# Four fused transformer layers on one core: a 64-column recurrence, first loads split over two queues, new order tables

## What is computed

```
x = L0(x, ctx)    # self-attention (16 heads of 64, causal) + cross-attention + FFN, three layer norms
x = L1(x, ctx)    # attention with 16 heads of 8, masked rows
x = L2(x, ctx)    # linear attention: one encoder layer on ctx, one decoder layer (8 heads of 16), FFNs
x = L3(x, ctx, base)   # attention with 8 heads of 16, then a recurrence over the 128 tokens
# the recurrence inside L3
U = (layernorm(x) @ W_in.T + b_in) @ Bmat
def step(s, u_t):                      # s is [32, 64]
    s = silu(s @ A.T) + u_t
    return s, s
_, states = scan(step, zeros, U)       # 128 steps, each needs the one before
out = x + einsum('tbs,sh->bth', states, Cmat) + mod
```

## Time and profile before

| | us |
|---|---|
| median of three runs | 2123.61 |
| profiled execution | 2124.64 |
| its span | 2122.9 |
| PE busy | 1872.6 (88%), 13625 matmuls |
| PE weight loads busy | 1198.0 (56%) |
| DVE busy | 1339.7 (63%) |
| ACT busy | 1109.4 (52%) |
| POOL busy | 239.0 (11%) |

### The profile page before, as it was taken

One profiled execution on the slowest core, in us unless ns is written; L12 is line 12 of the kernel. 1 busy time (PEld: TensorE's weight loads), 2 busy tenths in 40 slices (PEclk: granted clock), 3 DMA queues, 4 the chain that ended last, 5 costly groups with the idle time before them and its releaser, 6 DMA issues.

```text
span 2122.9 us, 36204 instructions
## 1 busy us (share of the span) xinstructions
PE 1872.6 (88%) x13625; PEld 1198.0 (56%) x13625; DVE 1339.7 (63%) x3612; ACT 1109.4 (52%) x3858; POOL 239.0 (11%) x263
## 2 busy tenths in 40 slices
PE   5887998899988998899988998899988998877699
PEld 2555565646655565546655565556655566544345
DVE  3554768577775768577775768577775768554410
ACT  3452845557363845557363845567473836433222
POOL 0001011010212011010212011010202011010000
PEclk9999999999999999999999999999999999988999
DMA  6000000000000000000000000000000000000001
GB/s 196 1 1 6 12 1 1 1 17 2 1 1 6 12 2 1 1 17 1 1 1 6 13 1 1 1 17 2 1 2 6 1 1 1 1 1 1 1 16 25
DMA packets 25138, 20.14 MB, mean 9 GB/s; under 512 B 2243, under 2 KB 22790, under 8 KB 24966
## 3 DMA queue, kind: packets, MB, share of 16 engines
q1 hardware_dynamic: 24966, 17.83, 2.9%
HBM read 15.73 MB, written 2.10 MB: 8 GB/s over the span
## 4 chain that ended last, share of the span: by engine, by line
PE 54%; DVE 23%; ACT 17%; issue 4%; POOL 2%; SPq 1%; DMA 0%; POOLq 0%; DVEq 0%; ACTq 0%
PE ps L825 12%; PE ps L833 11%; ACT probs L1474 7%; PE ps L873 5%; ACT s_probs L1474 4%; PE ps L974 3%; PE ps L897 3%; DVE neg_max L1735 3%; DVE tok L1755 3%; DVE stats L1742 3%; PE ps L883 2%; PE ps L998 2%; PE ps L1422 2%; PE ps L869 2%; PE ps L821 2%
## 5 line engine op out<-in xcount | busy, mean ns | idle before, releaser
L1474 ACT ACTIVATE probs<-ps,neg_max 128x128 f32<-128x128 f32 x1024 | 362.2, 395 | 147.7 <-DVE neg_max L1735 146.5
L1474 ACT ACTIVATION_READ_ACCUMULATOR probs<-ps,neg_max 128x1 f32 x1024 | 238.8, 234 | 0.0
L1474 ACT ACTIVATE s_probs<-ps,s_max 128x128 f32<-128x128 f32 x672 | 183.7, 396 | 95.6 <-DVE s_max L1735 95.6
L1735 DVE TENSOR_REDUCE neg_max<-ps 128x4 f32<-128x512 f32 x256 | 164.5, 684 | 89.8 <-PE ps L873 89.8
L647 POOL TENSOR_TENSOR rstd<-var_eps,minus_half 128x4 f32<-128x4 f32 x88 | 94.4, 1072 | 1068.0 <-DVE var_eps L1748 1067.2
L1742 DVE BATCH_NORM_STATS2 stats<-ps 128x6 f32<-128x128 f32 x352 | 78.2, 284 | 181.4 <-PE ps L833 179.6
L1777 DVE TENSOR_TENSOR probs<-probs,inv 128x512 f32<-128x512 f32 x256 | 177.1, 692 | 8.8
L1468 ACT ACTIVATE probsT<-ps 128x512 f32<-128x512 f32 (+1 forms) x270 | 164.2, 629 | 27.3 <-PE ps L883 13.6
L883 PE MATMUL ps<-ident,probs 128*128 128x128 f32 x1024 | 156.5, 281 | 8.6 <-ACT queries L1468 4.6
L873 PEld LDWEIGHTS ps<-keys,queries 64*128 64x128 f32 x2048 | 125.7, 189 | 54.7 <-issue 54.7
L873 PE MATMUL ps<-keys,queries 64*128 64x128 f32 x2048 | 150.5, 287 | 0.0
(11 more groups left out here) (296 smaller groups left out, 3421.8 us busy)
## 6 DMA issues: line engine op xcount, KB each, us to landing
x_in<-in_x SPq DMA_DIRECT2D x8, 256.0 KB, 3.0
c_in<-in_ctx SPq DMA_DIRECT2D x8, 256.0 KB, 3.2
skip_in<-in_mask_BxS_ik SPq DMA_DIRECT2D x8, 256.0 KB, 3.1
out<-headsT SPq DMA_DIRECT2D x28, 64.0 KB, 1.8
valid_in<-in_mask_BxS_bf SPq DMA_DIRECT2D x8, 64.0 KB, 3.7
w_qkv_sa<-in_L_xattn_sa_wq SPq DMA_DIRECT2D x1, 512.0 KB
w_qkv_sa<-in_L_xattn_sa_wk SPq DMA_DIRECT2D x1, 512.0 KB
w_qkv_sa<-in_L_xattn_sa_wv SPq DMA_DIRECT2D x1, 512.0 KB
```

The lines of the kernel that those rows point to most:

```text
L1474: last = A(dst[:, u % dst.shape[1], h * 128:h * 128 + 128], bank(st, (tag, "s", u))[:, h * 128:h * 128 + 128], ACT.Exp, bias=src_max[:, u ...
L1735: V.tensor_reduce(dst[:, u % 2, :], bank(st, (tag, "s", u)).rearrange("p (h k) -> p h k", h=4), AX.X, ALU.max, negate=True).then_inc(max_r ...
```

## The change

Three parts.

- **Recurrence.** All matmuls of it get weights of 64 columns: `scan_step` (only the 64 columns of `aT` that matter), the filler (`keep_half`), the states and the residual. The last two now take two time steps each in place of four and write 64 partitions of the bank, alternating between the lower and the upper half, so there are 64 of each in place of 32. The residual is no longer a transposition but an ordinary matmul with the identity. Even steps carry the states, odd steps the residual and a filler of 512 columns; the 768-column filler is gone but for the first step.
- **First loads.** The self-attention weights are loaded in halves (k, q and v of the first heads ahead of ctx, the rest behind), each with its own semaphore. The 8 vectors that are needed first, and the mask, are issued on ACT's queue; the other 26 stay on SP behind the self-attention weights. `col_rows` is transposed in two parts, the first before main step 1, the second before step 12. x, ctx and the mask have a semaphore each. ACT waits for the set-up steps only before its first projection, not before its first copy.
- **Order tables.** `MAIN_ORDER` and `SIDE_AT` are replaced. They hold the same items and the same 87 steps. They serve all eight passes.

```diff
-MAIN_ORDER = ("i0 av00 aq0 mk ak0 aq1 as0 ak1 av10 aq2 av01 as1 av11 av02 ax0 ak2 i1 ax1 aq3 ax2 at0 at1 as2 "
-              "av03 ak3 av12 ak4 ax3 at2 aq4 ax4 ao0 ax5 at3 as3 av13 ao1 ax6 at4 at5 ax7 aq5 at6 as4 ak5 aq6 "
-              "ao2 ak6 ax8 ax9 at7 as5 ao3 at8 ax10 at9 ax11 as6 ak7 ax12 aq7 at10 ao4 ax13 at11 as7 cv00 cv01 "
-              "ax14 ao5 at12 ax15 at13 cv02 at14 ao6 at15 ao7 y1 ck0 ck1 r1 n1 cv10 cv11 cq0 cv12 cs0 cv03 cx0 "
-              "cv13 cq1 cx1 cq2 ck2 cs1 ct0 cx2 ct1 cx3 cs2 cq3 ck3 co0 cq4 ct2 ct3 cx4 cx5 ck4 cs3 ck5 ct4 co1 "
-              "ct5 cx6 cx7 cs4 cq5 ck6 cx8 co2 cx9 ct6 cq6 ct7 ct8 cs5 cq7 co3 ct9 cx10 cs6 ck7 cx11 cx12 ct10 "
-              "co4 cx13 ct11 cs7 co5 cx14 cx15 ct12 ct13 ct14 co6 ct15 co7 y2 r2 n2 f0 f1 f2 f3 y3 r3 n3").split()
+MAIN_ORDER = ("i0 ak0 mk aq0 as0 av00 ak1 i1 ax0 av10 aq1 ax1 at0 as1 av01 av02 at1 ax2 ak2 aq2 av03 at2 as2 "
+              "ax3 ak3 ak4 ao0 aq3 ax4 av11 aq4 ax5 at3 as3 ao1 av12 av13 at4 at5 ax6 as4 ak5 ax7 ak6 at6 ao2 "
+              "aq5 at7 ax8 as5 ax9 ax10 aq6 ao3 at8 at9 at10 as6 ak7 ax11 aq7 cv00 ao4 at11 ax12 as7 cv01 ax13 "
+              "ao5 ax14 at12 at13 ax15 ck0 ao6 at14 at15 ao7 cv02 y1 cv10 ck1 r1 cv11 n1 cv12 cq0 cs0 cv03 cx0 "
+              "cq1 ck2 cx1 cv13 cs1 ck3 cx2 cq2 cq3 ct0 cx3 ct1 ct2 cs2 co0 ck4 cq4 cx4 ct3 cs3 co1 cq5 cx5 ck5 "
+              "ct4 cx6 ct5 cx7 cs4 ct6 cq6 co2 cx8 ct7 ct8 ck6 cs5 cx9 co3 ck7 cx10 ct9 cs6 cx11 co4 cq7 cx12 "
+              "ct10 ct11 cx13 cs7 co5 ct12 cx14 ct13 ct14 cx15 co6 ct15 co7 y2 r2 n2 f0 f1 f2 f3 y3 r3 n3").split()
...
-SIDE_AT = (0, 3, 4, 5, 8, 8, 10, 10, 12, 15, 16, 19, 21, 24, 26, 29, 33, 40, 42, 48, 49, 53, 56, 59, 62, 65,
...
+SIDE_AT = (3, 3, 4, 6, 6, 10, 14, 17, 18, 20, 20, 24, 27, 28, 30, 33, 39, 43, 48, 49, 53, 55, 55, 59, 62, 63,
...
+            load_x(0)
+            for c in "kqv":
+                load_sa(c, 0)
+            load_context(0)
+            for c in "kqv":
+                load_sa(c, 1)
+            for c in [*COLUMN_WIDTH][len(COLUMNS):]:
+                sp.dma_start(column_rows(c), column_source(c)).then_inc(loaded_vectors, 16)
...
-            pe.wait_ge(consts_ready, n_const[0])
-            pe.wait_ge(loaded_first, n_first[0])
-            nc.tensor.transpose(ps[:, 5, 0:NCOLS], col_rows[:, :], ident[0:NCOLS, 0:NCOLS]).then_inc(setup_filled, 1)
+            pe.wait_ge(consts_ready, IDENT_STEPS)
+
+            def turn_columns():
+
+                pe.wait_ge(consts_ready, n_const[0])
+                pe.wait_ge(loaded_columns, 16 * len(COLUMNS))
+                nc.tensor.transpose(ps[:, 5, 0:NFIRST], col_rows[0:NFIRST, :], ident[0:NFIRST, 0:NFIRST]).then_inc(setup_filled, 1)
...
-            aT = turned[:, TURN["L3_xattn_A", 0], :]
+            aT = turned[:, TURN["L3_xattn_A", 0], 0:NS]
+
+            def keep_half(halves, unused):
+
+                for n in range(0, halves, 2):
+                    width = 256 * min(2, halves - n)
+                    mm(ps[0:NS, unused, 0:width], ident_h[:, 0:NS],
+                       ident_h[:, :].unsqueeze(1).broadcast_to([128, width // 128, 128]), start=True, stop=True)
...
-                mm(ps[:, k % 2, 0:B], aT, scan_in[:, k - 1, :], start=True, stop=True).then_inc(scan_mm, 1)
...
+                mm(ps[0:NS, k % 2, 0:B], aT, scan_in[:, k - 1, :], start=True, stop=True).then_inc(scan_mm, 1)
...
+                last = mm(dst, final_rows(x2_all, m), ident[:, :], start=False, stop=True)
...
-                if k >= FINAL_STEPS and k % FINAL_STEPS == 0:
-                    final_states(k // FINAL_STEPS - 1)
-                elif k >= FINAL_STEPS and k % FINAL_STEPS == 1:
-                    final_residual(k // FINAL_STEPS - 1)
-                    keep_busy(2, 5)
+                if k >= 2 and k % 2 == 0:
+                    final_states(k // 2 - 1)
+                elif k >= 2:
+                    final_residual(k // 2 - 1)
+                    keep_half(2, 5)
                 else:
-                    keep_busy(3, 5)
+                    keep_half(3, 5)
...
-            act.wait_ge(setup_step, SETUP_FIRST)
+            for c in COLUMNS:
+                act.dma_start(column_rows(c), column_source(c)).then_inc(loaded_columns, 16)
+            act.dma_start(valid_in[:, :], I["mask_BxS2_bf1"].rearrange("b t -> (b t)")[0:GT].partition_broadcast(128)
+                          ).then_inc(valid_loaded, 16)
```

More of the change, by code:

```diff
@@ L276 @@
     NCOLS += _width
+NFIRST = sum(COLUMN_WIDTH[n] for n in COLUMNS)
 GB = {"ln1": ("L0_xattn_ln1_g", "L0_xattn_ln1_b"), "ln2": ("L0_xattn_ln2_g", "L0_xattn_ln2_b"),
@@ L461, in build_program @@
         prog_mean = sb("prog_mean", [NP, B])[:, :]
-        loaded_first = sem("loaded_first")
+        loaded_sa = {(c, part): sem(f"loaded_sa_{c}{part}") for c in "qkv" for part in range(2)}
+        loaded_columns = sem("loaded_columns")
+        loaded_vectors = sem("loaded_vectors")
         loaded_ca = sem("loaded_ca")
         loaded_rest = sem("loaded_rest")
-        group_in = sem("group_in")
+        x_loaded = sem("x_loaded")
+        context_loaded = sem("context_loaded")
+        valid_loaded = sem("valid_loaded")
         skip_loaded = sem("skip_loaded")
@@ L658, in main @@
                             wait_emptied(pool, i, MAIN, item)
+                            if i.g == 0 and item == ("in", 0):
+                                pool.wait_ge(setup_step, SETUP_FIRST)
                             carry_wait(8 + [*kept].index(item))
@@ L850, in project @@
                 x, source = {"sa": (xT["a"], ("in", 0)), "ca": (xT["b"], ("ln1", "n")) if kind == "q" else (cT, ("in", 1))}[tag]
+                if i.g == 0 and item in first_projections:
+                    pe.wait_ge(loaded_sa[first_projections[item]], N_SA[kind])
                 if i.g == 0 and item[1:] in (("k", 0), ("v", 0, 0)) and tag == "ca":
@@ L899, in outputs, with part_of @@
                 last.then_inc(filled[MAIN], 1)
-            def main(i):
-                for step in MAIN_STEPS:
+            def part_of(item):
+                return item[2] if item[1] == "v" else int(item[2] * 128 >= SA_PART[item[1]][1])
+            first_projections = {}
+            for item in (x for step in MAIN_STEPS for x in step if x[0] == "sa" and x[1] in ("q", "k", "v")):
+                if (item[1], part_of(item)) not in first_projections.values():
+                    first_projections[item] = item[1], part_of(item)
+            def main(i):
+                for n, step in enumerate(MAIN_STEPS):
+                    if i.g == 0 and n == COLUMNS_TURNED_AT:
+                        turn_columns()
+                    if i.g == 0 and n == VECTORS_TURNED_AT:
+                        turn_vectors()
                     for item in step:
@@ L1477, in exps @@
                 last.then_inc(emptied[st, "A"], 1)
+            first_column = next(item for step in MAIN_STEPS for item in step
+                                if item[1] in ("q", "k") and MAIN.by[item] == "A")
             def main(i):
@@ L1484, in main @@
                         tag, kind = item[:2]
+                        if i.g == 0 and item == first_column:
+                            act.wait_ge(setup_step, SETUP_FIRST)
                         if tag == "in":
@@ L1792, in make_masks, with keep_vectors @@
                 dve.wait_ge(masks_taken, i.at(1, 1))
+            def keep_vectors():
+                dve.wait_ge(setup_filled, 2)
+                link(once, setup_step, V.tensor_copy(col_all[:, NFIRST:NCOLS], ps[:, 6, NFIRST:NCOLS]))
             def main(i):
                 count[main_step] = 0
-                for step in MAIN_STEPS:
+                for n, step in enumerate(MAIN_STEPS):
+                    if i.g == 0 and n == VECTORS_TURNED_AT:
+                        keep_vectors()
                     for item in step:
```

93 lines of the change are left out of this document (54 added, 39 removed), and 6 rows, old and new, of the table SIDE_AT.

## The result

The changed kernel runs in 2092.19 us, the median of four runs (2088.1 to 2096.73), beside 2122.12 us for the kernel before on the same chip. The ratio is 0.9861, 95% interval 0.9834 to 0.9888: 30 us, 1.4% faster. In a later comparison the same code took 2090.39 us and the ratio was 0.9839 (0.9815 to 0.9863). The forecast was 2089 us.

The account below looks back on a forecast made before the run. PE was taken to bound the passes (busy 215.3 of 236.7 us), a chain the recurrence, loads not needed yet the start. Profiled 2124.6 - 13.4 (start) - 14.0 (recurrence) - 8 (tables) = 2089.2, forecast 2089 us, range 2068 to 2111.

Parts of the forecast that it names:

- Start, first projection: Kernel start: first projection at 8.2 instead of 21.64 us, behind the eight vectors' transposition; 13.4 us earlier (11.8 to 14.2).
- Start, the mask: First scores of the start: mask lands at about 9.7, scores may start at 12.4, PE waits 0.7 us.
- Start, SP's queue: Start: the other 26 vectors and cross-attention weights leave SP 2.5 us earlier, costed at nothing.
- Group 0 "at no change": Group 0, without a side stream and with waits for exponentials: the new tables were set at no change.
- Recurrence, the load: Scan step: two 64-column weight loads on the path save 2 x 0.060 = 0.119 us; 0.689 becomes 0.570, 15.1 us in all.
- Recurrence, odd steps: Odd scan steps: residual and filler overrun the shorter step by 0 to 0.04 us, taken as 0.016 in 63 steps, 1.0 us.
- Fast weight load: Recurrence: 128-column loads at 0.104 us are nearly as slow as float32 ones, so no fast load is lost; sum unchanged.
- Tables: Passes: PE's waits fall from 20.4 to 19.2 us, 1.2 per pass, 8.4 in seven, rounded to 8 us.
- A: Rival, passes: the new order costs up to 4 us per pass; 2104 to 2125 us; chance 0.15 if still faster.
- B: Rival, passes: the tables win much more, 3 us per pass (2076) or five (2062); chance 0.11 beyond the forecast.
- C: Rival, recurrence: one load on the path or odd steps overrun fully, 6 to 7.6 us won; 2096 to 2097; within forecast's 0.60.
- D: Rival, recurrence: the clock falls to its lower level, 42 us lost, total 2145; chance 0.08 together with a worse A.

Follow-up runs that it names:

- e2: The kernel before with only the first loads changed, old order tables and old recurrence: 2112.61 us, ratio 0.9939.
- e4: The changed kernel with the old order tables, so new first loads and recurrence only: 2098.35 us, ratio 0.9871.
- e5: The changed kernel with the first group's mask issued ahead of the eight vectors on ACT's queue: 2089.5 us, ratio 0.9835.
- e11: The changed kernel with the mask's load fourth on ACT's queue, behind three vectors and ahead of five: 2091.16 us, ratio 0.9838.
- e3: The kernel before with only the new order tables: 2117.04 us, ratio 0.9961.
- e6: The changed kernel with the recurrence's filler matmuls 128 columns wide again: 2105.48 us, ratio 0.9909.
- e1: The kernel before with only the recurrence's matmuls changed: 2110.3 us, ratio 0.9932.
- e0: The changed kernel itself run again, unedited, in the later comparison; its trace is the second trace: 2090.39 us, ratio 0.9839.
- e7: The changed kernel without the filler matmuls in the recurrence: 2107.34 us, ratio 0.9916.
- e9: The changed kernel with filler matmuls at two places of every pass where PE waits, around the L3 attention: 2090.14 us, ratio 0.9832.
- e12: The changed kernel with the mask's load first on ACT's queue and filler at two waits of the L3 attention: 2086.44 us, ratio 0.9838.

## Why the prediction was right

The forecast was 2089, the measurement 2092.19 and, later, 2090.39. The three terms of the sum, against the profiled execution and against the kernels with one part:

| | predicted | in the trace after | alone, by medians |
|---|---|---|---|
| start | 13.4 | 14.3 at the first projection, 8.0 at group 1 | 12.8 |
| recurrence | 14.0 | 13.5 less 0.2 behind it | 15.1 |
| tables | 8 | 4.7 in the seven passes | 8.4 |

- **Start, first projection.** 7.34 in place of 8.2. The path is right: behind the vectors, not behind x. The vectors' end was taken at 7.8 between 7.0 and 9.4; the trace has 7.1, the lower end. That it fell so near is in part luck: on ACT the eight issues took 2.8 us (0.78 to 3.57) where I took the 3.7 that they had on SP, so the last was issued at 3.25 and not at 4.2, but it took 3.9 us to land, not the 2.80 of the earlier trace rows. The table load ran beside the transpositions, so xT_a was ready at 5.9 and not at 7.0; it was not what PE waited for.
- **Start, the mask.** This step failed. I predicted a wait of 0.7 from the 5.2 of the earlier trace rows; the load took 7.0 (7.9 in the second trace) and PE waited 2.38 (3.8). The price of a landing was taken from a load with only x and ctx ahead of it, and used for one that is ninth on its queue while the self-attention weights are in flight on the other. My own terms didn't add up to 0.7 either: two projections at 1.86 us behind 8.2 end at 11.9, not 11.7.
- **Start, SP's queue.** I had SP reach the cross-attention weights 2.5 us earlier. It reaches them at 16.5, against 15.8 before: two of its issues now take 1.90 and 1.67 us. It cost nothing: PE has no wait for a load behind the eight vectors in group 0.
- **Group 0 "at no change"** failed: +6.3 in the trace. From the first projection to the transposition behind the first norm it takes 83.4 us (84.6 in the second trace) against 79.7 before, 78.5 and 79.1 with the early start and the old tables (e2, e4), 80.1 and 80.2 with the mask's wait gone (e5, e11). So the mask is 3 to 4 of it; the new list is about 1 by e5 and e11 against e4, 2.5 by e3 (82.2) against before. The other 2.6 lie behind that norm: 107.3 against 104.7. The same code has 103.3 there in the second trace, and the granted clock of 120 to 140 and of 140 to 160 differs (0.76 and 0.81 in the first, 0.83 and 1.00 in the second). That is scatter and not the change, as are the 1.9 us of the last group's side work (163.4 to 167.7 over all traces, in both directions).
- **Recurrence, the load.** Mechanism right, both loads on the path, term mis-sized: 2 x 0.060 = 0.119 predicted, 0.107 measured. The 0.060 was the difference between group totals of two other lines, whose single records have means of 143 and 136 ns, 7 apart. The records of the scan's own load give 188 - 134 = 54 ns, twice 0.054 = 0.108. The estimate that the Trainium skill gives ("TensorE: Matmul & The Clock Gate", LDWEIGHTS, columns/1.2) was 0.053 and 13.5 us, and that is what was measured: here the Trainium skill was closer than my rows.
- **Recurrence, odd steps.** I took 1.0 us for an overrun. There is none (0.582 for odd and even steps by silu's starts): the scan's load starts at 2041.71 beside the running filler. The load's error (15.1 for 13.5, +1.6) and this one (-1.0) mostly cancelled, so 14.0 against 13.3 looks better than its working was.
- **Fast weight load.** I weighed one rule of the Trainium skill ("TensorEngine Tiling (Array Packing)", Feature Incompatibilities: column tiling turns it off) and read from the group total of the earlier trace rows, 0.104 us, that there was no fast load to lose. That reading was wrong. Record by record, the filler's 128-column load takes 96 ns in e6_filler_128, half the 188 of the scan's float32 load of as many columns before, and less than the 111 of the 64-column load that replaced it. So by these records the wide load was the fast one, and narrowing lost it: 15 ns in 63 odd steps, 0.9 us if nothing covered it. It is covered, as odd and even steps both take 0.582. The group total hid this, as it is mostly of loads that run beside matmuls. The rule of the Trainium skill that mattered ("TensorEngine Tiling (Array Packing)", Tiling Modes, Key Properties) is the one on draining, and I did not weigh it. It was harmless only because the change narrowed every matmul of the stretch: 10.3 us otherwise (e6).
- **Tables.** The count of PE's waits, 1.2 us per pass, is near what passes without a dip show: 1.3, of it 0.85 in idle time. Named waits, predicted and measured: cross-attention scores 0.75 and 0.87, xT_a 0.65 and 0.69, L3 scores 1.16 and 1.20, the norm after d1's FFN 1.1 and 1.20. The d0 query was predicted at 0.9 and has 1.45; the norm after the encoder's FFN was predicted at 0.75 and doesn't wait. What I had no term for is the dip: three of the first six passes of this trace are longer than 235.2 by 2.8, 1.6 and 2.8 us, 7.2 in all, against 2.0 over the first six of before; the seventh passes have 0.3 and 1.0. That is why the trace shows 4.7 and not 9.1, and part of why its execution is the slowest of four. Over all traces the passes win more than in this one: seven take 1658.5 to 1663.4 us in the four kernels with the old tables (before, e1, e2, e4) and 1647.8 to 1653.8 in the seven traces with both new ones and the same work (after, e0, e3, e5, e6, e7, e11). The means are 1662.0 and 1650.3, 11.6 us apart: the term of 8 was small for the passes, and group 0 gives a part back.
- **Rivals.** A and B are out: passes without a dip win 1.3 us, the means over all traces 1.7 per pass; none loses 1 or wins 3. C is out: both loads counted. D did not occur (clock 1.00), but its mechanism is real (e7), at a price of 14 us without the filler. Its 42 us were for the low clock with the filler still in the stretch, a case that no run had.

## What to carry to other kernels

Price a narrower weight load from the record of that very instruction, and count it only where the loads are on the chain; then narrow every matmul of the stretch, the filler too, or the changes of width cost most of what the loads win (here 10.3 of 13.5 us). An early start is worth only what the next load in line leaves of it, so ask for the second and third thing that PE will need and not for the first alone, and ask again when the order behind it changes. Sort passes by their granted clock before comparing them: a dip of 3 us in one pass hides a gain of 1.3 in another.

## What the runs showed of the hardware that I had not expected

- Going from 64-column to 128-column weights and back within a step cost 0.165 us (odd steps of e6 0.747 against 0.582): 0.22 with the residual in the lower half of the bank, 0.11 with it in the upper half.
- The record of a bfloat16 weight load of 128 columns takes 96 ns (e6), less than one of 64 columns (111 ns, after); in float32 it is 188 for 128 columns (before) and 134 for 64 (after).
- Without the filler, with a scan pair and an output pair in every step, the granted clock of the recurrence fell to 0.50 and stayed there (e7). With one filler of 512 columns more in every other step it was 1.00.
- With the new tables the dips of the clock in the passes sit behind one cluster of waits: 13 of 14 dips in seven traces (after, e0, e3, e5, e6, e7, e11) start 203 to 204 us into a pass. 1.6 us of filler inside two of these waits left none in the fourteen passes of two traces (e9, e12).
- A 2 KB load behind a 64 KB broadcast on one queue landed 7 us after its issue (e11), and a 256 KB load took 4.9 and 5.2 in place of 3.0 us in the two kernels where the broadcast had been issued on another queue in the same instant (e12, e5).
